# Late rows of expert 0 in two fp32r parts at fixed columns, token table at tile 27, routing in three places per batch

## What is computed

```python
h = x @ W[cat] + b[cat]                    # conditioning, 4096 x 512
probs = softmax(h @ Wr); e = argmax(probs) # 8 experts
rank = number of earlier tokens with the same expert; keep = rank < 512
ye = relu(h[dispatch] @ W1[e]) @ W2[e]     # 512 -> 2048 -> 512, 512 slots per expert
y[token] = ye * prob (dropped tokens: 0)
out = x + y
```

## Time and profile before

| | us |
|---|---|
| median of 3 runs | 827.72 (827.39 to 828.08) |
| the profiled execution | 827.8 |
| its span | 826.1 |
| TensorE busy | 819.2 (99%) |
| VectorE busy | 403.9 (49%) |
| ScalarE busy | 252.0 (31%) |
| GpSimd busy | 229.9 (28%) |
| L1023, first layer, 1536 products | 352.5, mean 389 ns |
| L1004, second layer, 1536 products | 352.1, mean 389 ns |
| L918, conditioning, 336 products | 83.3 |
| L971, late rows, 24 products | 5.8, mean 391 ns |

### The profile page before, as it was taken

How to read it: one execution, slowest core, us unless ns; L and a number is a source line. 1 busy time by engine, 2 the same in 40 slices (tenths; PEclk the granted TensorE clock), 3 DMA queues, 4 the chain that set the end, 5 groups by cost and what they waited for, 6 DMA issues and landing times.

```text
span 826.1 us, 10815 instructions
## 1 busy us (share of the span) xinstructions
PE 819.2 (99%) x4119; PEld 673.0 (81%) x4119; DVE 403.9 (49%) x556; ACT 252.0 (31%) x345; POOL 229.9 (28%) x238
## 2 busy tenths in 40 slices
PE   9999999999999999999999999999999999999997
PEld 6777887888888888888888888888888888888886
DVE  4677746443545346532744164425443455337531
ACT  3422205331333224321533053304332233214320
POOL 2000117245302730173107420553036401030201
PEclk9999999999999999999999999999999999999999
DMA  8985644734373425332534444434534363215101
GB/s 291 365 328 182 238 129 150 253 127 128 103 253 119 138 80 208 132 131 102 157 147 143 149 165 152 134 133 131 212 124 130 98 240 115 99 66 200 54 0 51
DMA packets 61098, 127.18 MB, mean 154 GB/s; under 512 B 8300, under 2 KB 8300, under 8 KB 60562
## 3 DMA queue, kind: packets, MB, share of 16 engines
q1 hardware_dynamic: 47570, 94.93, 32.4%
q0 software_dynamic: 13216, 31.42, 11.7%
q10 hardware_dynamic: 288, 0.52, 0.2%
HBM read 110.13 MB, written 25.17 MB: 164 GB/s over the span
## 4 chain that ended last, share of the span: by engine, by line
PE 99%; DMA 1%; issue 0%; ACT 0%; POOL 0%; DVE 0%; SPq 0%; POOLq 0%
PE acc_ps L1023 42%; PE y_ps L1004 42%; PE acc_ps L918 7%; PE tp_ps L918 3%; PE tp_ps L837 1%; PE y_ps L971 1%; PE acc_ps L902 1%; PE tp_ps L819 0%; PE y_ps L878 0%; DMA stage<-cond_w 0%; PE y_ps L902 0%; PE tp_ps L902 0%; PE y_ps L977 0%; PE acc_ps L906 0%; DMA cat_sb<-cat 0%
## 5 line engine op out<-in xcount | busy, mean ns | idle before, releaser
L1023 PE MATMUL acc_ps<-xt_split,w_split 128*128 128x512 f32 x1536 | 352.5, 389 | 0.3 <-ACT xt_split L535 0.3
L1004 PE MATMUL y_ps<-w_split,xt_split 128*128 128x512 f32 x1536 | 352.1, 389 | 0.0
L1023 PEld LDWEIGHTS acc_ps<-xt_split,w_split 128*128 128x128 f32 x1536 | 288.1, 188 | 60.7 <-ACT xt_split L535 0.5
L1004 PEld LDWEIGHTS y_ps<-w_split,xt_split 128*128 128x128 f32 x1536 | 288.3, 188 | 59.9
L548 ACT ACTIVATE xt_split<-acc_ps 128x512 fp32r<-128x512 f32 x128 | 76.5, 598 | 415.6 <-PE acc_ps L1023 415.6
L771 DVE SCALAR_TENSOR_TENSOR xt_split<-acc_ps,xt_split 128x512 fp32r<-128x512 f32 x128 | 88.6, 692 | 205.9 <-ACT xt_split L548 205.9
L405 POOL DMA_INDIRECT rows<-h_rows,idx_all x112 | 116.5, 1040 | 254.6 <-DVE tp_ps L761 215.3
L794 DVE SCALAR_TENSOR_TENSOR rows<-y_ps,p_cur,rows 128x512 f32<-128x512 f32 x32 | 24.0, 751 | 133.0 <-PE y_ps L1004 133.0
L676 DVE TENSOR_TENSOR w_split<-stage,w_split 128x1024 fp32r<-128x1024 f32 x66 | 81.0, 1227 | 16.4 <-ACT w_split L496 16.4
L682 DVE TENSOR_TENSOR w_split<-stage,w_split 128x1024 fp32r<-128x1024 f32 x64 | 78.5, 1227 | 16.4 <-ACT w_split L502 16.4
L443 POOL DMA_INDIRECT out<-rows,put_all x32 | 31.4, 982 | 154.3 <-DVE rows L794 154.3
(11 more groups left out here) (123 smaller groups left out, 243.1 us busy)
## 6 DMA issues: line engine op xcount, KB each, us to landing
stage<-w SPq DMA_DIRECT2D x64, 1024.0 KB, 5.6
b_rows<-x SPq DMA_DIRECT2D x8, 1024.0 KB, 7.8
h_rows<-rows POOLq DMA_DIRECT2D x6, 1024.0 KB, 8.3
stage<-cond_wt SPq DMA_DIRECT2D x4, 1024.0 KB, 8.8
x_more<-x_t SPq DMA_DIRECT2D x4, 1024.0 KB, 8.4
stage<-x_t SPq DMA_DIRECT2D x3, 1024.0 KB, 8.0
stage<-cond_w SPq DMA_DIRECT2D x3, 1024.0 KB
h_rows<-rows SPq DMA_DIRECT2D x8, 256.0 KB, 2.3
```

Of the source, the lines that this page charges most:

```text
L1004: last = nc.tensor.matmul(y_ps[:, s, :], hts[:, j % HB, a, s * P:(s + 1) * P], w2s[:, q % 2, w, jj, :], start=(j == 0 and (a, w) == (HI, HI)),
L1023: last = nc.tensor.matmul(acc_ps[:, j % 2, :], w1s[slot][:, w, k, jj * P:(jj + 1) * P], xts[:, par, a, k, :], start=(k == 0 and (w, a) == ...
```

## The change

- **Late rows.** ScalarE copies each of the three late tiles from `rows` to a high part (`late_rows[HI]`), and VectorE makes the low part (`split_late`, at tiles 29, 30, 31). Both lie in a free quarter of `xt_split`. The selection matrix covers all 512 slots and is fp32r, in the low part of a w1 buffer. `add_late` multiplies each part with it at fixed columns. The window, its eight products and the register loads go.
- **Tables.** The token table is made after tile 27 (`make_tokens`); the others and the quarter lists follow on VectorE behind the splits of the first expert's rows. `spread_all` comes on TensorE behind `add_early(3)`.
- **Routing.** `route` handles both chunks of a batch in one place into one 256-column area, with one copy by ScalarE. `m_turn` stands beside `by_token` (tiles 8, 13, 18), `rank_of` beside `m_sum` (10, 15, 20), `fill_table` beside `by_token` (13, 18, 23). Some splits move by one or two tiles.
- **Start.** Only block 0 of the first x chunk is loaded from ScalarE's queue. Blocks 1 to 3 come from SyncE's, each ahead of its weight block. The splits take x and weight blocks in turn. 12 warm-up products instead of 14.

```diff
-    M_TURN = [4, 9, 14, 19]
+    M_TURN = [4, 8, 13, 18]
     M_SUM = [5, 10, 15, 20]
-    ROUTE = [6, 7, 11, 12, 16, 17, 21, 22]
+    ROUTE = [6, 11, 16, 21]
     CHOOSE = [8, 13, 18, 23]
-    PLACE = [9, 14, 19, 25]
-    FILL = [11, 16, 21, 27]
+    PLACE = [10, 15, 20, 25]
+    FILL = [13, 18, 23, 27]
-    SPLIT_X = [None, None, (3, 4), (6, 7), (10, 11), (15, 16), (20, 21), (22, 24)]
-    SPLIT_W = [None, (4, 4, 5, 5), (10, 11, 12, 12), (16, 17, 17, 20)]
-    KEEP_FIRST = 14
+    SPLIT_X = [None, None, (3, 4), (6, 7), (12, 14), (16, 17), (21, 22), (22, 24)]
+    SPLIT_W = [None, (4, 4, 5, 5), (11, 11, 12, 13), (16, 17, 18, 19)]
+    KEEP_FIRST = 12
-    SPLIT_W1 = [NT - 8, NT - 5]
+    SPLIT_W1 = [NT - 8, NT - 4]
+        late_rows = xts[:, 1, :, :, :]
+        late_sel = w1s[1][:, LO, 0:LATE, :]
-        idx_ps = y_ps[:, 1, 0:NQ * E * SB].rearrange("p (q e s) -> p q e s", q=NQ, e=E)
+        idx_ps = tp_ps[:, 0, 2 * P:2 * P + NQ * E * SB].rearrange("p (q e s) -> p q e s", q=NQ, e=E)
-        turn_ps = tp_ps[:, 0, 0:P]
+        turn_ps = y_ps[:, 3, 2 * P:3 * P]
+        logits_ps = tp_ps[:, 0, 0:CPB * P]
...
             for k in range(DK):
-                if k >= DK // 2:
+                if k >= 1:
                     sp.dma_start(stage[:, 2, k, :], xt_v[:, k, 0:CH]).then_inc(s_x0[k], 16)
                 sp.dma_start(stage[:, 1, k, :], cond_view(0)[:, k, :]).then_inc(s_w0[k], 16)
...
-            for k in range(DK // 2):
-                act.dma_start(stage[:, 2, k, :], xt_v[:, k, 0:CH]).then_inc(s_x0[k], 16)
-            for k, w in ((0, None), (1, 0), (2, 1), (3, 2), (None, 3)):
-                if k is not None:
-                    split_first(k)
-                if w is not None:
-                    split_cond(0, w)
+            act.dma_start(stage[:, 2, 0, :], xt_v[:, 0, 0:CH]).then_inc(s_x0[0], 16)
+            for k in range(DK):
+                split_first(k)
+                split_cond(0, k)
...
+            for i in range(LATE):
+                act.wait_ge(s_accf, NT - LATE + i + 1)
+                nc.scalar.activation(late_rows[:, HI, i, :], rows[:, 1, TPC - LATE + i, :], ACTF.Copy
+                                     ).then_inc(s_latehi, 1)
...
-                then(nc.vector.tensor_scalar(window[:, :], base_ps, float(CAP - P), None, ALU.min))
-                nc.vector.tensor_copy(window_at[0:1, :], window[0:1, :]).then_inc(s_win, 1)
...
                 for i in range(LATE):
-                    last = nc.vector.tensor_scalar(late_sel[:, i, :], iota_c[:, 0:P], late_rel[:, i:i + 1], None,
+                    last = nc.vector.tensor_scalar(late_sel[:, i, :], iota_c[:, :], late_rel[:, i:i + 1], None,
                                                    ALU.is_equal)
                 last.then_inc(s_late, 1)
+
+            def split_late(i):
+                dve.wait_ge(s_latehi, i + 1)
+                nc.vector.tensor_tensor(late_rows[:, LO, i, :], rows[:, 1, TPC - LATE + i, :],
+                                        late_rows[:, HI, i, :].bitcast(f32), ALU.subtract).then_inc(s_latelo, 1)
...
-                if n == PLACE[-1]:
+                if n == PLACE[-1] + 1:
                     choose_late()
-                if n == NT - 2:
-                    spread_quarters()
+                if n == FILL[-1]:
+                    make_tokens()
+                if n >= NT - LATE:
+                    split_late(n - (NT - LATE))
...
             for k in range(DK):
                 split_xe(k, 0, k, y_ps[:, k, :])
+            make_tables()
+            spread_quarters()
...
+            def route(b):
+
+                pe.wait_ge(s_mcopy, b + 1)
+                if b >= 1:
+                    pe.wait_ge(s_ltc, b)
+                for h in range(CPB):
+                    c = CPB * b + h
+                    if c >= 1:
+                        pe.wait_ge(s_xin[c % 4], 16 * (c // 4 + (c % 4 > 0)))
+                    for k in range(DK):
+                        for g in range(NQ):
+                            last = nc.tensor.matmul(logits_ps[g * G:(g + 1) * G, h * P:(h + 1) * P], m32[:, b % 2, k, :],
+                                                    x_in[c % 4][:, k, g * P:(g + 1) * P],
+                                                    start=(k == 0), stop=(k == DK - 1))
+                    last.then_inc(s_lt, 1)
...
-                if b == BATCH - 1:
-                    for t in range(TPB - 1):
-                        i = max(0, t + 1 - (TPB - LATE))
-                        nc.tensor.matmul(base_ps[:, i:], ones[:, :], onehot[:, t, 0:1].to_broadcast([P, LATE - i]),
-                                         start=(t == 0), stop=False)
-                    last = nc.tensor.matmul(base_ps, ones[:, :], count[:, b % 2, 0:1].to_broadcast([P, LATE]),
-                                            start=False, stop=True)
...
-                if n in FILL:
-                    fill_table(FILL.index(n))
+                if n in CHOOSE:
+                    by_token(CHOOSE.index(n))
...
-                if n == NT - 3:
-                    pe.wait_ge(s_win, 1)
-                    at = [pe.value_load(window_at[0:1, i:i + 1], min_val=0, max_val=CAP - P) for i in range(LATE)]
-                if n == NT - 2:
-                    spread_all()
...
             def add_late(i):
-                pe.wait_ge(s_accf, NT - LATE + i + 1)
-                for k in range(DK):
-                    nc.tensor.matmul(y_ps[:, k, bass.ds(at[i], P)], by_block(rows[:, 1, TPC - LATE + i, :], k),
-                                     late_sel[:, i, :], start=(i == 0), stop=False, skip_group_check=True)
+                for half in (HI, LO):
+                    pe.wait_ge((s_latehi, s_latelo)[half], i + 1)
+                    for k in range(DK):
+                        nc.tensor.matmul(y_ps[:, k, :], by_block(late_rows[:, half, i, :], k), late_sel[:, i, :],
+                                         start=(i == 0 and half == HI), stop=False, skip_group_check=True)
...
             pe.wait_ge(s_late, 1)
-            pe.wait_ge(s_quart, 1)
+            pe.wait_ge(s_tok, 1)
             add_late(0)
...
             add_early(3)
+            spread_all()
```

More of the change, by code:

```diff
@@ L127, in moe_kernel @@
         late_rel = sb("late_rel", [P, LATE], f32)
-        window = sb("window", [P, LATE], f32)
-        window_at = sb("window_at", [1, LATE], mybir.dt.int32)
-        late_sel = sb("late_sel", [P, LATE, P], f32)
         put_all = sb("put_all", [P, E, SB], u32)
@@ L590, in copy_m @@
                 if b >= 2:
-                    dve.wait_ge(s_ltc, CPB * (b - 1))
+                    dve.wait_ge(s_ltc, b - 1)
                 if b == 0:
@@ L661, in choose_late @@
                 late = slice(NT - LATE, NT)
[L662 to L667 removed]
+                then(nc.vector.tensor_scalar(late_rel[:, :], onehot[:, TPB - LATE:, 0], -float(SKIP), float(SKIP),
+                                             ALU.mult, ALU.add))
+                then(nc.vector.tensor_tensor(late_rel[:, :], late_rel[:, :], place_all[:, late], ALU.add))
                 for i in range(LATE):
[L669 removed]
+                    last = nc.vector.tensor_scalar(late_sel[:, i, :], iota_c[:, :], late_rel[:, i:i + 1], None,
                                                    ALU.is_equal)
                 last.then_inc(s_late, 1)
+            def split_late(i):
+                dve.wait_ge(s_latehi, i + 1)
+                nc.vector.tensor_tensor(late_rows[:, LO, i, :], rows[:, 1, TPC - LATE + i, :],
+                                        late_rows[:, HI, i, :].bitcast(f32), ALU.subtract).then_inc(s_latelo, 1)
             def split_w1(half, count, slot):
@@ L826, in m_sum @@
                 nc.tensor.transpose(m_ps, m_rows[:, :], ident[:, :]).then_inc(s_m, 1)
-            def route(c):
-                pe.wait_ge(s_mcopy, c // CPB + 1)
-                if c >= 1:
-                    pe.wait_ge(s_xin[c % 4], 16 * (c // 4 + (c % 4 > 0)))
-                if c % CPB:
-                    pe.wait_ge(s_ltc, c)
-                for k in range(DK):
-                    for g in range(NQ):
-                        last = nc.tensor.matmul(turn_ps[g * G:(g + 1) * G, :], m32[:, (c // CPB) % 2, k, :],
-                                                x_in[c % 4][:, k, g * P:(g + 1) * P],
-                                                start=(k == 0), stop=(k == DK - 1))
-                last.then_inc(s_lt, 1)
+            def route(b):
[12 more added lines that the diff above has]
+                    last.then_inc(s_lt, 1)
             def by_token(b):
-                pe.wait_ge(s_ltc, CPB * (b + 1))
+                pe.wait_ge(s_ltc, b + 1)
                 if b >= 1:
```

30 lines of the change are left out of this document (12 added, 18 removed).

## The result

The changed kernel takes 825.87 us (median of 15 runs, 825.37 to 826.54), the kernel before 827.56 (15 runs, 827.19 to 828.08). The ratio is 0.998 with a 95% interval of 0.9972 to 0.9987: faster by 1.69 us. The forecast was 826.1, with -1.61 us as its sum.

A forecast was written before the change was run, and what follows sets the result against it. TensorE was taken to bound the kernel, ending the chain for 99% of the span. -2.41 + 0.10 + 0.70 = -1.61 us against 827.8 gave 826.2, and 826.1 as median; range 824.9 to 827.9, the forecast case's own 825.4 to 826.8.

The forecast's parts named there:

- tile 4 to late rows: TensorE's tile phase: fewer breaks and group entries, base products and spread removed; -2.41 us, bounds 1.14 to 2.77 saved.
- late products: 24 late-row products on TensorE, now fp32r on 512 columns: 5.44 us against 5.45, plus one 0.13 break; +0.1.
- the rest up to the second layer, with the spread: Spread moved behind the early rows, covered before the first expert product; cost 0, upper bound 0.81 us.
- start: Second x block issued later from SyncE delays chunk 1, so tile 4 is late by 0.70 us; bounds 0 to 1.0.
- the price of a break: Where small groups interrupt the tiles: 0.13 us for the tile behind, 0.09 for entering a group of 32-column weights.
- I take no loss: Late products' strided fp32r weight loads, 326 ns against 188, were taken to overlap the products; loss 0.
- the bound of 2.4: Upper bound in us for the late products, 24 x (326 - 227), if a strided weight load sets the pace.
- the slower rival: Strided loads of the 24 late products not hidden: +0.8 us, 828.5 (chance 0.08), or +6.2, 833.9 (0.04).
- 119 ns pace: Equally strided transposes of L977 follow each other every 119 ns with loads of 219; taken as evidence that loads overlap.
- the pacing of the first tile: First 96 expert products took 22.33 us instead of 21.76, paced by the splits; unpaced start due at 125.08.
- the empty hole at 3 to 4 us: DMA window that carried the second x block at 264 GB/s; would stay empty, putting 0.26 MB ahead of chunk 1.
- Hidden, with some 4 us left: Quarter gathers on GpSimd start about 4 us later behind the late tables; covered by VectorE's 8.10 us idle.

The follow-up runs named there:

- routes_apart: Changed kernel with each double route taken apart again, one tile between the two; tile 4 to late rows 97.63 us against the changed kernel's 96.19.
- spread30: Changed kernel with the spread on TensorE behind tile 30 again, as before; one run 827.38 us, tile 4 to late rows 97.13 us, +0.94.
- late_fp32: Changed kernel with the late rows as before (fp32, 128-column window, base products, register loads); tile 4 to late rows 96.41 us, +0.22.
- late_contig: Changed kernel with the late rows' parts stored block by block, so weight loads read consecutive elements; 826.21 us against 827.70 for the kernel before.
- before_new_start: Kernel before with the new start alone; 828.17 us against 827.70, ratio 1.0005 (0.9996 to 1.0014).
- x1_scalar: Changed kernel with the second x block back on ScalarE's queue; chunk 1 used at 13.77 us, tile 4 at 17.97.
- x1_scalar_b: Same edit to the changed kernel, second x block on ScalarE's queue, run again; 836.38 us, ratio 0.9972 to the kernel before, tile 4 at 19.21.
- after_again: The changed kernel itself run once more, on the other chip; 834.78 us beside 836.06 for the kernel before, ratio 0.9981 (0.995 to 1.0011).

## Why the prediction came out as it did

| step | predicted, us | measured, us |
|---|---|---|
| tile 4 to late rows | -2.41 | -2.32 |
| late products | +0.10 | +0.39 |
| the rest up to the second layer, with the spread | 0 | -0.05 |
| start | +0.70 | -0.09 in the profile, +0.47 timed by itself |
| sum | -1.61 | -2.07 in the profile; -1.51 with +0.47; -1.69 by the medians |

That the sum came within 0.1 us of the measured 1.69 is in part luck: the late products were put 0.29 too low and the start at least 0.23 too high, and the two cancel.

**Tile phase.** Right in sum, and its parts can now be told: the four merged route pairs -1.44 (routes_apart), the spread with its break -0.94 (spread30), the base products -0.22 (late_fp32), together -2.60. So the three other merged breaks gave back 0.28 where I had them at -0.39. Two pairs of small groups show where. The two transposes of `by_token` took 0.14 ahead of a tile, and ahead of `m_turn` they take 0.31 (35.53 to 35.84); `m_sum` took 0.03 ahead of a tile and takes 0.11 ahead of `rank_of` (42.47 to 42.58). With three of each that is 0.51 + 0.24 = 0.75, which less the 0.39 leaves +0.36, near the 0.28. So what a small group costs depends on what follows it, and in my sum two errors cancelled: the price of a break was too low for equal groups and too high for unlike ones.

**Late products.** The mis-sized term. "I take no loss" for the strided load was wrong by 0.28 us, 12 ns a product (late_contig); the bound of 2.4 was far off too, and the slower rival that stood on it falls. The 119 ns pace of the strided transposes had ruled out a large penalty, and that is what the products showed: most of a load of 312 ns still lies under the product before it. The Trainium skill's 16-byte line rule ("SBUF — State Buffer", section Door 1) names the penalty rightly: the load takes 312 ns strided and 188 contiguous. How much of it the products hide, only the runs tell.

**Spread.** Right, and closer than its working says. Of the 0.57 that I took for the pacing of the first tile, some 0.16 is only the chain's way of counting a product behind a wait (22.33 by the chain, 22.17 from start to start). So the spread had nothing to spare, where I had 0.12; the measured rest of -0.05 and spread30's +0.93 say that it was covered all the same.

**Start.** This is the step that failed. It was described rightly from chunk 1 on, and before_new_start shows its very times. The size failed in two ways. Timed by itself it is +0.47, not +0.70. And it was taken as a constant, where the landing of chunk 1 varies by up to 1.24 us between executions of one kernel. Whether the empty hole at 3 to 4 us, and so the queue of the second block, is its cause stays open: the middles say 0.45, the single executions overlap, and x1_scalar and x1_scalar_b lie at the two ends. The Trainium skill's rule that I weighed ("DMA: Bandwidth & Descriptors", Issuing engines are not separate DMA queues) would have given +0.43; the timed 0.47 lies next to it, but its interval reaches from below nothing to past 0.70 (0.9996 to 1.0014 of 827.7 is -0.3 to +1.2), so no run here decides between the rule and my sum.

**Cover of the gathers.** "Hidden, with some 4 us left" was right in its first word only; 1.1 us was left. The gathers start 4.5 us later against the loop (5.02 behind its first product, 0.53 before), near the forecast of 4. But the transposes come 8.1 us later (155.91, which is 33.16 behind the first product, against 149.60, 25.09 behind it), and GpSimd's signal that all quarters are there, which VectorE needn't wait for in the kernel before, comes 9.4 later (at 155.9 against 148.3, or 33.15 behind the first product against 23.79). I counted the delay of the issue and not what it would meet. The last quarter's gather is issued at 148.79, among SyncE's three loads, and is there 7.1 us later; before, it was issued at 145.42, 4.4 us ahead of those loads, and was there 2.9 us later. The other profiles show that the loads are the cause. In after_again, the same kernel, a pause held the loads back until 157.15. Its GpSimd and SyncE timelines, and the signal:

```profile
148.64 1.00 POOL L405 DMA_INDIRECT rows<-h_rows,idx_all  x1 [0.30 <-issue]
```

```profile
157.15 0.37 SPq L242 DMA_DIRECT2D stage<-w  x1
```

```profile
L430 POOLq EVENT_SEMAPHORE  x1: 17/17/17, 151.3 to 151.3; - x1
```

There the last quarter was in place 2.7 us after its issue. Over all fourteen profiles it is 2.5 to 2.9 us in the five where the loads were issued after the signal, and 5.8 to 7.2 us in the nine where they were issued before it.

## What to carry to other kernels

Small products between large ones are priced by their neighbours: equal groups put together save more than the gaps (0.36 us a pair here), unlike ones can lose it again, so price each pair from the profile rather than with one mean. When a late step moves behind others, ask which transfers its own transfer will now share the DMA engines with, and count the cover that is left from the landing that this gives, not from the issue. And where an effect hangs on the landing of one load early on, read its time from several executions before believing either sign.

## What the runs showed of the hardware

- A strided fp32r weight load (every fourth element) takes 312 ns against 188, but adds only 9 to 18 ns to a stream of 512-column products (236 against 227, 259 against 241).
- 64 fp32 products with 32-column weights in one group take 1.88 us, two groups of 32 take 1.01 each.
- An idle stretch of TensorE of 2.81 us, after over 100 us of steady work, was followed by a granted clock of 0.77, 0.50 and 0.88 in three windows of 2 us, which cost another 1.74 us from start to start. The shorter pauses ahead of tile 4 in these kernels (0.16 to 1.07 us) left the granted clock at 1.00 in the window from 16 to 22 us.
- The time at which the same early load was in place scattered from 13.77 to 15.01 us over 14 executions of kernels with two forms of the start, and by 1.24 us between two executions of one of them.
- The last of sixteen indirect gathers of GpSimd was in place 2.5 to 2.9 us after its issue when SyncE's three loads of 1 MB came later (five executions), and 5.8 to 7.2 us after it when they were issued around it or up to 6.2 us ahead of it (nine executions).
